# All units of the residual product of both residual attention layers issued ahead of the first tile of the aggregation

## The chip, the cores and the metric

The kernel runs on one core of a Trainium2 chip, as one launch. A core has a matrix engine (TensorE, PE in the profile), a vector engine (VectorE, DVE), a scalar engine (ScalarE, ACT), GpSimd (POOL) and a queue engine that issues transfers (SyncE, SP). Each runs its own instruction stream in order; streams meet only at semaphores. The metric is the device time of one execution in microseconds, the median over the runs shown.

## The reference

A chain of four graph networks over 625 nodes with 768 features; each adds its result to its input and normalises the rows. The first is a relational convolution, the second a plain graph convolution; the change touches neither. The third has two attention layers with a residual product each, and the change is there:

```python
h = gat_conv(x, edge_index, W1, a_src1, a_dst1, b1, HEADS, HID, True)      # 4 heads of 256
h = relu(layer_norm(h, g1, be1)) + (h0 @ Wr1 + br1)                        # residual product, 768 x 1024
h1 = h
h = gat_conv(h, edge_index, W2, a_src2, a_dst2, b2, 1, OUT_DIM, False)     # 1 head of 768
h = layer_norm(h, g2, be2) + (h1 @ Wr2 + br2)                              # residual product, 1024 x 768
# gat_conv: softmax over the edges that end in a node of leaky_relu(alpha_src + alpha_dst),
# then the sum of the source nodes' feature rows with these weights
```

The fourth network has two attention layers without a residual product (Q2 and Q3 in the kernel).

## The kernel before

Nodes are cut into NB = 5 blocks of BP = 125. Products in full precision are made of three matmuls on halves of the operands (high times low weight, low times high, high times high; lines 2060, 2063, 2064). Weights come as chunks of 128 rows by up to 384 columns through a ring of ten slots: SP loads a chunk, ACT makes its high half (`split_hi`, line 1065), POOL its low half (`split_to`, line 766), and PE waits for the low half and reports a used slot with `w_used`.

The two residual layers are the objects Q0 (first layer, 4 heads) and Q1 (second layer, 1 head). In each, PE goes through these steps:

- the feature product, with the attention scores beside it;
- the residual product in **units** (`residual_unit`): one unit is one block of nodes times one column piece. Q0 has 15 units of 6 chunks, i.e. 18 matmuls (units 0 to 9 are 384 columns wide, 10 to 14 are 256), Q1 has 10 units of 8 chunks, 24 matmuls. Q0's units use PSUM banks 3 and 4 in turn up to unit 9, and bank 3 alone from unit 10; Q1's alternate to the end. ACT copies a finished unit from its bank to `resid` (`residual_read`, line 1135), and POOL adds a bias row (`q0_residual`, line 806) or the layer's input (`q1_residual`, line 840);
- the aggregation in **tiles**: a tile of scores is a head and a block of nodes (20 in Q0, 5 in Q1). DVE writes the tile (`steep_or_flat`, line 1885), PE transposes its five blocks (`turn_tile`, line 2475), ACT takes exponentials in PSUM (`exps`, line 1087), DVE multiplies with the edge counts (`probs`, line 1848), and PE sums (`sum_tile`, line 2486: 5 matmuls for a Q0 tile, 10 for a Q1 tile). DVE inverts the row sum (`z`, line 1857), and ACT copies the scaled sum out (`out_scaled`, line 1148).

In Q0, PE turns tile j + 3 right after it sums tile j; DVE makes the last part of a tile's probabilities only after the sum of the tile before. After every fourth tile a block of nodes is complete: DVE takes statistics, ACT a square root (its table and that of the exponential are loaded in turn, lines 1026 and 1087) and the normalisation (line 1032), POOL multiplies by the gain (`q0_gain`, line 797), DVE adds and makes the layer's output (`q0_out`, lines 1874 and 1876). From tile 13 on PE also transposes the finished blocks for Q1 (`turn_x8`, line 2527), six of them through bank 4 alone, each after DVE has read the one before (line 1862). In Q1, each tile completes a block: read, statistics, square root, normalisation, gain (line 845), addition of the residual (line 1930), a second normalisation, and the transpose for Q2 (`turn_x2`, line 2049), which PE has between the two units of a later tile.

Before the change, PE has units 0 to 3 of Q0 ahead of the first tile, and the others each behind a tile, as a table says; in Q1 units 0 to 4 stand ahead and one unit before each tile. ACT's reads and POOL's additions follow that order by hand:

```python
Q0_BESIDE = {0: (4,), 1: (5,), 2: (6,), 3: (7,), 4: (8,), 5: (9,), 6: (10,), 7: (11,), 8: (12,), 10: (13,), 12: (14,)}
```

A queue limit matters: POOL splits the weight chunks of the second piece after it has added to unit 4 and those of the third after unit 9; ACT splits high halves just before it reads units 4, 9 and 14.

## Time and profile before

| | |
|---|---|
| time before, three runs | 1610.96 us median (1610.59 to 1614.87) |
| profiled execution, its own time | 1607.97 us |
| its span in the trace | 1606.2 us |
| mean granted clock of TensorE | 0.954 of full speed |
| busy: PE, DVE, POOL, ACT | 1464.7, 791.7, 506.6, 427.4 us |
| Q0's tile loop up to the sum of tile 13 | 1059.14 to 1134.87 us |
| Q0's tiles 13 to 19, with the transposes for Q1 | 1134.87 to 1181.56 us |
| Q1's units 0 to 5, then its tile loop | 1244.53 to 1270.23, 1270.23 to 1321.49 us |

Times are microseconds from the span's start. "Busy" is the time in which an engine has an instruction running; PE's matmuls overlap, so a matmul's duration is longer than the distance to the next start, and distances between starts are what a sequence costs. "PEclk" is the clock that TensorE was granted, 1.00 being 2.4 GHz and 0.50 being 1.2 GHz.

### The profile page before, as it was taken

Reading aid. Unit: us, or ns where it says so; the run is one execution under the profiler, and the core shown is the slowest. Engines: PE = TensorE matmul, PEld = TensorE weight load, DVE = VectorE, ACT = ScalarE, POOL = GpSimd, SP = SyncE. Lnnn points to the kernel's source line nnn. Section 1 sums busy time; section 2 is a strip of 40 time slices with the busy share of each in tenths; the row PEclk is TensorE's granted clock in tenths of the full one; section 3 lists DMA queues with packets and bytes.
Section 4 is the critical chain, followed back from the end, with each engine's and each line's share of the span. In section 5 each row is a group of like instructions: output and inputs, shape, how many; then the busy total and the mean of one; then the engine's idle time right before and its main releaser. Section 6 shows DMA issues by size and latency. Waiting matters only on the chain.

```text
span 1606.2 us, 23414 instructions
## 1 busy us (share of the span) xinstructions
PE 1464.7 (91%) x8072; PEld 1343.7 (84%) x8072; DVE 791.7 (49%) x1940; ACT 427.4 (27%) x1009; POOL 506.6 (32%) x586
## 2 busy tenths in 40 slices
PE   5899699999999999999999998999688998878896
PEld 3566699999999999999998997898578867767773
DVE  7889644224443365642324435534534043678524
ACT  1153511111000001101003113345524333544422
POOL 5110332423334424434342420633226534100020
PEclk9999899999999999999999998999889999777998
DMA  3110111213343243422112211310012102000001
GB/s 113 41 30 9 37 45 30 60 32 82 89 132 105 63 116 84 123 74 60 55 50 59 60 30 41 87 58 26 20 47 81 49 5 84 16 1 1 10 1 48
DMA packets 57656, 86.53 MB, mean 54 GB/s; under 512 B 6442, under 2 KB 54183, under 8 KB 57433
## 3 DMA queue, kind: packets, MB, share of 16 engines
q1 hardware_dynamic: 45184, 66.02, 14.3%
q10 hardware_dynamic: 12374, 19.17, 4.1%
q8 instruction: 66, 1.08, 0.3%
q14 instruction: 32, 0.26, 0.1%
HBM read 83.24 MB, written 1.92 MB: 53 GB/s over the span
## 4 chain that ended last, share of the span: by engine, by line
PE 74%; DVE 14%; ACT 5%; issue 4%; POOL 1%; DMA 1%; DVEq 0%; ACTq 0%; SPq 0%; POOLq 0%
PE psum L2060 13%; PE psum L2064 12%; PE psum L2063 12%; PE psum L2486 7%; PE psum L2077 7%; PE psum L2080 7%; PE psum L2165 2%; PE psum L2401 1%; PE psum L2406 1%; PE psum L2405 1%; ACT psum L1087 1%; DVE onehot_dst L1370 1%; PE psum L2121 1%; PE psum L2475 1%; PE psum L2457 1%
## 5 line engine op out<-in xcount | busy, mean ns | idle before, releaser
L2060 PE MATMUL psum<-w_lo,xT_hi 128*125 128x384 f32 (+2 forms) x1200 | 412.1, 343 | 11.7 <-POOL w_lo L766 5.3
L2063 PE MATMUL psum<-w_hi,xT_lo 128*125 128x384 f32 (+2 forms) x1200 | 405.5, 338 | 0.0
L2064 PE MATMUL psum<-w_hi,xT_hi 128*125 128x384 f32 (+2 forms) x1200 | 405.0, 337 | 0.0
L753 POOL CAST w_hi<-w_raw 128x384 fp32r<-128x384 f32 x190 | 103.3, 544 | 502.4 <-PE psum L2064 492.3
L2060 PEld LDWEIGHTS psum<-w_lo,xT_hi 128*125 128x125 f32 (+1 forms) x1200 | 225.0, 187 | 16.5 <-POOL w_lo L766 8.3
L766 POOL TENSOR_TENSOR w_lo<-w_raw,w_hi 128x384 fp32r<-128x384 f32 x106 | 109.8, 1065 | 387.9 <-ACT w_hi L1065 277.1
L2063 PEld LDWEIGHTS psum<-w_hi,xT_lo 128*125 128x125 f32 (+1 forms) x1200 | 225.4, 188 | 0.1
L2064 PEld LDWEIGHTS psum<-w_hi,xT_hi 128*125 128x125 f32 (+1 forms) x1200 | 224.8, 187 | 0.0
L1406 DVE TENSOR_TENSOR h_lo<-psum,h_hi 125x384 fp32r<-125x384 f32 (+1 forms) x120 | 66.9, 558 | 316.1 <-ACT h_hi L923 315.1
L2077 PE MATMUL psum<-h_lo,adjacency 125*125 125x384 f32 (+3 forms) x600 | 204.1, 340 | 1.8 <-ACT adjacency L963 1.7
L755 POOL TENSOR_TENSOR w_lo<-w_raw,w_hi 128x384 fp32r<-128x384 f32 x190 | 200.8, 1057 | 15.2
L923 ACT ACTIVATE h_hi<-psum 125x384 fp32r<-125x384 f32 (+1 forms) x120 | 59.0, 491 | 545.3 <-PE psum L2064 540.9
L2080 PE MATMUL psum<-h_hi,adjacency 125*125 125x384 f32 (+3 forms) x600 | 203.4, 339 | 0.0
L2486 PE MATMUL psum<-features,score_tiles 125*125 125x257 f32 (+2 forms) x400 | 122.6, 461 | 4.4 <-DVEq L2012 3.1
L2077 PEld LDWEIGHTS psum<-h_lo,adjacency 125*125 125x125 f32 (+1 forms) x600 | 112.0, 187 | 3.2 <-ACT adjacency L963 2.3
L1087 ACT ACTIVATE psum<-psum,al_src_slope 125x125 f32<-125x125 f32 x350 | 94.7, 351 | 73.9 <-PE psum L2475 73.8
L2080 PEld LDWEIGHTS psum<-h_hi,adjacency 125*125 125x125 f32 (+1 forms) x600 | 112.5, 188 | 0.3
L2486 PEld LDWEIGHTS psum<-features,score_tiles 125*125 125x125 f32 x400 | 79.2, 202 | 36.6 <-issue 5.0
L2486 PE MATMUL psum<-features,more_tiles 125*125 125x97 f32 x400 | 68.5, 334 | 26.1 <-DVE more_tiles L1848 25.9
L2486 PEld LDWEIGHTS psum<-features,more_tiles 125*125 125x125 f32 x400 | 63.5, 246 | 30.1 <-DVE more_tiles L1848 30.0
L2165 PE MATMUL psum<-onehot_dst,onehot_src 128*125 128x512 bf16 x336 | 62.5, 326 | 6.3 <-DVE onehot_dst L1370 5.9
L1370 DVE TENSOR_SCALAR onehot_dst<-iota,dst_of_pair 128x625 bf16<-128x625 f16 x168 | 62.8, 410 | 9.7 <-PE psum L2165 9.7
(286 smaller groups left out, 2097.9 us busy)
## 6 DMA issues: line engine op xcount, KB each, us to landing
w_raw<-weights_dram SPq DMA_DIRECT2D x296, 192.0 KB, 2.4
score_w_raw<-weights_dram ACTq DMA_DIRECT2D x58, 192.0 KB, 2.9
x_nat<-x_dram SPq DMA_DIRECT2D x1, 1875.0 KB
x_residual<-x_dram SPq DMA_DIRECT2D x1, 1875.0 KB
out_dram<-x_residual SPq DMA_DIRECT2D x5, 375.0 KB
score_a_rows<-L_gnn_a_src_dram ACTq DMA_DIRECT2D x8, 192.0 KB, 3.4
score_a_rows<-L_gnn_a_dst_dram ACTq DMA_DIRECT2D x8, 192.0 KB, 5.1
rgcn_bias<-rgcn_bias_dram SPq DMA_DIRECT2D x1, 1125.0 KB
```

Source lines behind the costliest of these rows:

```text
L753: nc.gpsimd.tensor_copy(mem.wh[:, slot, :], mem.raw[:, raw_slot, :]).then_inc(w_hi_ready, 1)
L755: nc.gpsimd.tensor_tensor(mem.wl[:, slot, :], mem.raw[:, raw_slot, :], mem.wh[:, slot, :].bitcast(F32), ALU.subtract).then_inc(w_lo_ready, 1)
L766: nc.gpsimd.tensor_tensor(mem.wl[:, c % WRING, :], mem.raw[:, c % RAW, :], mem.wh[:, c % WRING, :].bitcast(F32), ALU.subtract).then_inc(w_ ...
L1087: ins = nc.scalar.activation(t, t, ACT.Exp, bias=mem.al_src2[0:BP, n % NB, h:h + 1])
L1370: nc.vector.tensor_scalar(mem.oh_dst[:, n % OH_RING, 0:N], mem.iota[:, 0:N], mem.dst_pair[:, s % 2, j:j + 1], None, ALU.is_equal).then_inc ...
L2060: ins = nc.tensor.matmul(o, h, wl, start=(j == 0), stop=False, skip_group_check=True)
L2063: nc.tensor.matmul(o, l, wh, start=False, stop=False, skip_group_check=True)
L2064: ins = nc.tensor.matmul(o, h, wh, start=False, stop=stop and j == k - 1, skip_group_check=True)
L2077: ins = nc.tensor.matmul(o, a, mem.hl[0:p, slot, 0:width], start=(s == 0), stop=False, skip_group_check=True)
L2080: ins = nc.tensor.matmul(o, a, mem.hh[0:p, slot, 0:width], start=False, stop=(s == NB - 1), skip_group_check=True)
L2165: ins = nc.tensor.matmul(o, mem.oh_src[:, t, 0:BP], mem.oh_dst[:, n % OH_RING, w:w + 512 if w == 0 else NC], start=False, stop=(t == GROUP ...
L2486: ins = nc.tensor.matmul(bank(q.out_bank(u), off, off + width), blocks(p_tile(q, j))[:, k, :], feat_flat(q, k, a, a + width), start=(k == ...
```

## The change

On PE, units 4 to 14 of Q0 now stand between unit 3 and the sum of tile 0, and the table goes; units 5 to 9 of Q1 all stand ahead of its tile 0. ACT reads the units in the same new order, and has one group of high halves at tile 8 rather than 17. POOL adds to all units first, then splits, then has the gains.

```diff
@@ POOL
             for i in range(NB * len(Q0.pieces)):
-                if i == 10:
-                    q0_gain(0)
-                elif i == 13:
-                    q0_gain(1)
                 q0_residual(i)
                 if i == 4:
                     split_to(Q0.chunk + 32)
                 elif i == 9:
                     split_to(Q0.end)
             split_to(Q0.end + 4)
-            q0_gain(2)
-            q0_gain(3)
+            for b in range(3):
+                q0_gain(b)
             split_to(Q0.end + AHEAD)
-            q0_gain(4)
+            for b in range(3, NB):
+                q0_gain(b)
...
             for b in range(NB):
                 q1_residual(b)
-                if b:
-                    q1_gain(b - 1)
             split_to(Q1.end + 4)
+            for b in range(NB - 1):
+                q1_gain(b)
             q1_gain(NB - 1)
@@ ACT
-            residual_read(Q0, 2)
-            residual_read(Q0, 3)
+            for i in range(2, NB * len(Q0.pieces)):
+                residual_read(Q0, i)
...
-                for i in Q0_BESIDE.get(j, ()):
-                    residual_read(Q0, i)
...
-                if j == 17:
+                if j == 8:
                     split_hi(Q0.end + AHEAD)
...
-            for i in range(NB):
+            for i in range(2 * NB):
                 residual_read(Q1, i)
             for s in range(NB + 2):
                 if s < NB:
-                    residual_read(Q1, NB + s)
                     q1_read(s, 0)
@@ PE
-            for i, tiles in ((0, (0, 1)), (1, (2,)), (2, ()), (3, ())):
+            for i in range(NB * len(Q0.pieces)):
                 residual_unit(Q0, mem.xh, mem.xl, i)
-                for j in tiles:
-                    turn_tile(Q0, j)
+                if i == 0:
+                    turn_tile(Q0, 0)
+                    turn_tile(Q0, 1)
+                elif i == 1:
+                    turn_tile(Q0, 2)
             for j in range(4 * NB):
                 sum_tile(Q0, j)
                 if j + 3 < 4 * NB:
                     turn_tile(Q0, j + 3)
-                for i in Q0_BESIDE.get(j, ()):
-                    residual_unit(Q0, mem.xh, mem.xl, i)
...
+            for i in range(NB, 2 * NB):
+                residual_unit(Q1, mem.xh8, mem.xl8, i)
             for b in range(NB):
-                residual_unit(Q1, mem.xh8, mem.xl8, NB + b)
                 sum_tile(Q1, b, (lambda: turn_x2(b - 2)) if b >= 2 else None)
```

PE's rows in Q0, from the sum of tile 0 on. Before, the sum and the transposes of tile 3 are followed by the 18 matmuls of unit 4 (the first four are shown):

```order
L2486 MATMUL psum<-features,score_tiles 125x257 [waits feat_biased,gemm_read,prob_ready]
L2486 MATMUL psum<-features,score_tiles 125x257 x4
L2475 MATMUL psum<-ident,score_tiles 125x125 [waits g_ready]
L2475 MATMUL psum<-ident,score_tiles 125x125 [waits prob_ready]
L2475 MATMUL psum<-ident,score_tiles 125x125 x3
L2060 MATMUL psum<-w_lo,xT_hi 125x384 [waits gemm_read]
L2063 MATMUL psum<-w_hi,xT_lo 125x384
L2064 MATMUL psum<-w_hi,xT_hi 125x384
L2060 MATMUL psum<-w_lo,xT_hi 125x384
```

With the change, the last matmuls of unit 14 stand ahead of the same sum, and the tiles' rows follow each other with no product between them:

```order
L2053 MATMUL psum<-w_lo,xT_hi 125x256
L2056 MATMUL psum<-w_hi,xT_lo 125x256
L2057 MATMUL psum<-w_hi,xT_hi 125x256
L2479 MATMUL psum<-features,score_tiles 125x257 [waits feat_biased,gemm_read,prob_ready]
L2479 MATMUL psum<-features,score_tiles 125x257 x4
L2468 MATMUL psum<-ident,score_tiles 125x125 [waits g_ready]
L2468 MATMUL psum<-ident,score_tiles 125x125 [waits prob_ready]
L2468 MATMUL psum<-ident,score_tiles 125x125 x3
L2479 MATMUL psum<-features,score_tiles 125x257 [waits prob_ready]
L2479 MATMUL psum<-features,score_tiles 125x257 x4
L2468 MATMUL psum<-ident,score_tiles 125x125 [waits prob_ready,g_ready]
```

So 11 units, 198 matmuls, moved from behind tiles 0 to 8, 10 and 12 to ahead of tile 0; each sum now waits on `prob_ready` right behind the transposes.

POOL's rows in Q0, from the additions to units 0 to 4 (`br_first`) on. Before, two gains stand among the additions:

```order
L806 TENSOR_TENSOR residual_product<-residual_product,br_first 125x384 [waits gemm_read] x5
L766 TENSOR_TENSOR w_lo<-w_raw,w_hi 128x384 [waits w_hi_ready] x6
L806 TENSOR_TENSOR residual_product<-residual_product,br_rest 125x384 [waits br1_loaded,gemm_read]
L806 TENSOR_TENSOR residual_product<-residual_product,br_rest 125x384 [waits gemm_read] x4
L766 TENSOR_TENSOR w_lo<-w_raw,w_hi 128x384 [waits w_hi_ready] x4
L797 TENSOR_TENSOR dest_even<-dest_even,par_141 125x1024 [waits normed2]
L806 TENSOR_TENSOR residual_product<-residual_product,br_rest 125x256 [waits gemm_read] x3
L797 TENSOR_TENSOR par_142<-par_142,par_141 125x1024 [waits normed2]
L806 TENSOR_TENSOR residual_product<-residual_product,br_rest 125x256 [waits gemm_read] x2
```

With the change:

```order
L805 TENSOR_TENSOR residual_product<-residual_product,br_first 125x384 [waits gemm_read] x5
L765 TENSOR_TENSOR w_lo<-w_raw,w_hi 128x384 [waits w_hi_ready] x6
L805 TENSOR_TENSOR residual_product<-residual_product,br_rest 125x384 [waits br1_loaded,gemm_read]
L805 TENSOR_TENSOR residual_product<-residual_product,br_rest 125x384 [waits gemm_read] x4
L765 TENSOR_TENSOR w_lo<-w_raw,w_hi 128x384 [waits w_hi_ready] x4
L805 TENSOR_TENSOR residual_product<-residual_product,br_rest 125x256 [waits gemm_read] x5
L765 TENSOR_TENSOR w_lo<-w_raw,w_hi 128x384 [waits w_hi_ready] x4
L796 TENSOR_TENSOR dest_even<-dest_even,par_141 125x1024 [waits normed2]
```

The gains moved behind all additions; the two groups of low halves (`w_lo`, x6 and x4) stay behind the additions to units 4 and 9 in both.

## Rows read from the trace of the kernel before

**Rows 1.** Busy time by stage: length, each engine's busy time, granted clock, DMA.

```profile
1059.14:1134.87 75.73, 70.18 (x395) 63.42 (x394) 32.07 (x72) 40.54 (x112) 24.68 (x23) 0.95 0.11 34
1134.87:1181.56 46.69, 28.85 (x117) 23.24 (x115) 15.97 (x36) 20.23 (x47) 14.26 (x12) 0.78 0.14 38
...
1244.53:1270.23 25.70, 25.66 (x145) 25.34 (x146) 0.87 (x2) 7.56 (x19) 16.32 (x14) 1.00 0.23 64
1270.23:1321.49 51.26, 51.26 (x215) 37.15 (x214) 18.32 (x56) 20.78 (x39) 15.76 (x9) 1.00 0.02 7
1321.49:1340.16 18.67, 10.21 (x49) 9.24 (x50) 10.39 (x23) 7.26 (x15) 12.32 (x11) 0.82 0.32 91
```

**Rows 2.** PE's longest group of waits from 1059 to 1182 us: total, times, longest.

```profile
PE psum L2527 <- DVE x8T_lo L1862: 17.4, 5, 4.8
```

**Rows 3.** Timeline of PE in Q0's tile loop: start, length, instruction, idle before.

```profile
1061.78 0.42 PE L2060 MATMUL psum<-w_lo,xT_hi 128*125 128x384 f32 x1
...
1065.01 2.33 PE L2486 MATMUL psum<-features,score_tiles 125*125 125x257 f32 x10
...
1103.15 0.57 PE L2060 MATMUL psum<-w_lo,xT_hi 128*125 128x256 f32 x1 [2.83 <-POOL w_lo L766]
...
1106.82 3.50 PE L2486 MATMUL psum<-features,score_tiles 125*125 125x257 f32 x10
...
1110.62 0.36 PE L2060 MATMUL psum<-w_lo,xT_hi 128*125 128x256 f32 x1
...
1112.83 2.33 PE L2486 MATMUL psum<-features,score_tiles 125*125 125x257 f32 x10
...
1117.68 2.33 PE L2486 MATMUL psum<-features,score_tiles 125*125 125x257 f32 x10
...
1121.12 2.33 PE L2486 MATMUL psum<-features,score_tiles 125*125 125x257 f32 x10
...
1138.74 2.33 PE L2486 MATMUL psum<-features,score_tiles 125*125 125x257 f32 x10
...
1144.85 2.33 PE L2486 MATMUL psum<-features,score_tiles 125*125 125x257 f32 x10
...
1152.02 4.49 PE L2486 MATMUL psum<-features,score_tiles 125*125 125x257 f32 x10
```

**Rows 4.** Timeline of POOL at unit 4's addition and the splits behind it.

```profile
1066.74 1.00 POOL L806 TENSOR_TENSOR residual_product<-residual_product,br_first 125x384 f32<-125x384 f32 x1 [5.84 <-ACT residual_product L1135]
1067.70 5.12 POOL L766 TENSOR_TENSOR w_lo<-w_raw,w_hi 128x384 fp32r<-128x384 f32 x5
```

**Rows 5.** Timeline of DVE: the end of a block, score tiles, probabilities.

```profile
1112.33 1.23 DVE L1876 SCALAR_TENSOR_TENSOR residual_product<-dest_even,residual_product 125x1024 f32<-125x1024 f32 x1
...
1117.00 0.61 DVE L1885 TENSOR_SCALAR score_tiles<-score_tiles,row_steep,row_flat 125x625 f32<-125x625 f32 x1
...
1124.77 2.33 DVE L1885 TENSOR_SCALAR score_tiles<-score_tiles,row_steep,row_flat 125x625 f32<-125x625 f32 x1
...
1128.42 0.72 DVE L1848 SCALAR_TENSOR_TENSOR score_tiles<-psum,counts_loops 125x125 f32<-125x125 f32 x2
```

**Rows 6.** Timelines of ACT and POOL: the second block's square root, normalisation and gain.

```profile
1118.28 1.28 ACT L1026 ACT_TABLE_LOAD   x1
...
1123.04 1.25 ACT L1032 ACTIVATE par<-par,ln_shift,ln_std 125x1024 f32<-125x1024 f32 x1
1124.37 2.38 POOL L797 TENSOR_TENSOR par<-par,par 125x1024 f32<-125x1024 f32 x1 [5.31 <-ACT par L1032]
```

**Rows 7.** Timeline of ACT in Q1: tile 3's first read, and the last normalisations of tiles 3 and 4.

```profile
1306.88 0.58 ACT L1148 ACTIVATE x_residual<-psum,z 125x384 f32<-125x384 f32 x1 [1.93 <-POOL residual_product L840]
...
1315.16 1.03 ACT L1032 ACTIVATE x_residual<-x_residual,ln_shift,ln_std 125x768 f32<-125x768 f32 x1 [0.42 <-DVE ln_shift L1513]
...
1329.62 1.03 ACT L1032 ACTIVATE x_residual<-x_residual,ln_shift,ln_std 125x768 f32<-125x768 f32 x1 [0.43 <-DVE ln_shift L1513]
```

**Rows 8.** Busy time from 1117 to 1134 us, columns as in Rows 1.

```profile
1117.00:1134.00 17.00, 15.60 (x97) 13.80 (x96) 11.96 (x26) 11.77 (x32) 4.03 (x3) 1.00 0.01 1
```

More of the change, by code:

```diff
@@ L607, in program @@
         X8_BANKS = [4] * 6 + [5, 6, 7, 4]
-        Q0_BESIDE = {0: (4,), 1: (5,), 2: (6,), 3: (7,), 4: (8,), 5: (9,), 6: (10,), 7: (11,), 8: (12,), 10: (13,), 12: (14,)}
         X8_AT = {13: 0, 14: 1, 15: 2, 16: 3, 17: 4, 18: 5, 20: 6, 21: 7, 24: 8, 25: 9}
```

## The prediction

> **What bounds the kernel now.** I read the stages first, and asked of each that the change touches whether PE works or waits there, then the list of PE's waits, then the timelines. Q0's loop up to the sum of tile 13 lasts 75.73 us, and PE is busy for 70.18 of them. The next six tiles take 46.69 us with PE busy for 28.85 at a mean clock of 0.78: there PE waits. In Q1 PE has no gap at all in units 0 to 5 (25.70 us) and in the tile loop behind them (51.26 us); then come 18.67 us with PE busy for 10.21 [rows 1]. PE's waits say on what: 17.4 us in five waits of the transposes for Q1 for the reader of bank 4 [rows 2], all from tile 14 on; the longest single wait before that is 2.83 us on a low half of the weights, at unit 10 [rows 3]. So units between tiles are what fills PE while DVE and ACT work on the scores. The change takes no work away; it takes this filling from where there is other work to wait for.
>
> **Q0, units 4 to 14 ahead of tile 0.** A 384-wide unit costs 3.23 us from start to start (1061.78 to 1065.01), a 256-wide one 2.21 (1110.62 to 1112.83) [rows 3]: 6 x 3.23 + 5 x 2.21 = 30.4 us, the same as before. What is added:
> - Low halves at unit 5. POOL adds to unit 4 (1.0 us) before it splits chunks 26 to 29, at 1.02 us each [rows 4]. ACT's read first, about 0.6: the first half is there 2.6 us after unit 4, the fourth 5.7, and three matmuls (0.5) end unit 5 at 6.3 instead of 3.2. Wait 3.1 us. Before, a tile lay between and took most of it.
> - The same at unit 10. From unit 9's start, ACT and POOL need 2.0 us for the split that POOL has before its additions; five additions take it to 7, the four splits to 11.1, the last matmuls to 11.5. Without waits units 9 and 10 take 5.4. Wait 6.1 us. Before, with a tile between, the longest piece of it was 2.83 [rows 3].
> - Bank 3 alone for units 10 to 14: each of the last four must let ACT read its predecessor, 0.4 us and two hand-overs, 0.65 us. Four times: 2.6 us, between 0 and 4.
> - The clock. Behind the wait of 2.83 us the sum of tile 7 took 3.50 us rather than 2.33 [rows 3]: TensorE was at 1.2 GHz. Behind a wait of about 4 us the same falls on units 10 to 12: 2 us, between 0 and 5.
>
> The new stretch ahead of tile 0: 30.4 + 3.1 + 6.1 + 2.6 + 2.0 = 44.2 us.
>
> **Q0, tiles 0 to 12 bare.** PE's own work for a tile is the sum and five transposes, 2.64 us (from tile 0's sum at 1059.14 to unit 4 at 1061.78) [rows 1, 3]. The rest of the loop sets a longer beat. (a) DVE makes a tile's last probabilities after the sum of the tile before: a sum starts 2.33 us for its predecessor, a hand-over, the inverse and the first of two parts of 0.36 [rows 5] after the last one, about 2.8. (b) Every fourth tile the last transpose waits for a bank: tile 9 to tile 10, which had no unit between, took 3.44 us (1117.68 to 1121.12) [rows 3]. Four plain tiles: 2.85 + 3.44 + 2.63 + 2.8 = 11.7 us. (c) Once a block is complete, ACT loads a table (1.28 us), takes the root, loads the other table (1.28), makes exponentials and normalises (1.25); POOL multiplies (2.38); DVE needs two operations of 1.2 and only then writes the next score tile (0.61), on which PE's transposes wait [rows 5, 6]. I walked tiles 4 to 12 through the four queues with these durations: exponentials come 0.8 us late at the third tile behind a block's end, and at the fourth DVE's output is 1.4 us late for the transposes. Tiles 4 to 7 take 12.5 us, 8 to 11 take 13.7, tile 12 takes 4.2. Sum 11.7 + 12.5 + 13.7 + 4.2 = 42.1 us, 3.24 a tile. Bounds: 2.63 a tile, PE's own work (34.2), and 3.87 a tile, the step from tile 13's sum (1134.87, the end of the stretch) to tile 14's at 1138.74, which holds a transpose for Q1 too (50.3) [rows 1, 3]. I take the walk; it lies between (a) and the measured 3.87.
>
> Q0 to tile 13: 44.2 + 42.1 = 86.3 against 75.73: **+10.6 us**. The six tiles after it depend on the same chain as before; ACT comes 0.8 us later into it: **+0.8**. ACT's five high halves at tile 8 (2.2 us) and POOL's splits between gains lie in slack there and cost nothing; if tile 8's exponentials were late for them, it would be 2 us.
>
> The Trainium skill has a rule on this loop (SBUF — State Buffer, Who interferes with whom): DVE and GpSimd share a port pair, and the one that comes second is blocked for the other's whole instruction. The trace agrees: a score tile took 2.33 us beside POOL's gain and 0.61 otherwise [rows 5, 6]. By it, POOL's additions leaving the loop would relieve DVE, while a gain that fell beside each block's score tile would cost 1.7 us four times. My walk has DVE waiting for the gain, so neither is added.
>
> **Q1, units 5 to 9 ahead.** Six units took 25.70 us [rows 1], 4.28 each, so tile 0 starts 4 x 4.22 = 16.9 us later; the work is PE's either way. A tile then costs PE 6.4 to 6.9 us instead of 11. But each completes a block, and its chain is serial: from ACT's first read (1306.88) through turns, statistics, two normalisations and the second read to the end of the last normalisation (1316.19) is 9.3 us, the gain beside it [rows 7]. Before, that hid beneath 11 us of PE. Now from tile 0's start: last normalisation of tile 0 at 10.3, of tile 1 at 19.5, then 9.3 a tile, of tile 4 at 47.4. That is 16.9 + 47.4 = 64.3 us from the old start of the loop (1270.23), where it was at 60.4 (1329.62 + 1.03) [rows 7]: **+3.9 us**, and what follows (splits, turns, products of Q2) hangs on it as before. Bounds: 0, if all of it hides, and 9.3, if one more beat is missed. The longer gaps, up to 5 us, may leave the products behind them at 1.2 GHz: **+1**, between 0 and 3.5.
>
> Weights: Q1's second piece is asked for at the same place as before, and POOL's additions no longer stand before tiles 1 to 4. SP's queue only follows the low halves. Costless.
>
> **Sum.** 10.6 + 0.8 + 3.9 + 1.0 = 16.3 us. The profiled execution took 1607.97 us, so 1624.3; the median of the runs shown is 3.0 higher, so I forecast **1627 us**. A change within 0.3%, 4.8 us, is about what a measurement of this kernel can't tell from none.
>
> **Rivals.**
> - *TensorE falls to half clock in the bare loop.* A sum at 1.2 GHz is the 4.49 us of 1152.02, 2.2 more than at 2.4 GHz [rows 3]. If half of the 13 tiles run so: +14 us, 1641. For it: the loop would have PE idle a fifth of the time, and the six tiles that are already bare have 0.78. Against: 1117 to 1134 had PE idle for 1.4 of 17 us and stayed at 1.00 [rows 8]. Chance 0.17. The Trainium skill (TensorE: Matmul & The Clock Gate, A second HAM failure mode) describes just this, frequent short idling between groups of matmuls making the clock swing; no full-clock row here has as much idling as the new loop.
> - *Hidden anyway, no change.* The bare loop runs at PE's 2.63 a tile (-7.9 us), the clock holds (-3), and Q1's chain hides (-3.9): +1.5, 1612. Against: (a) and (b) are order, not luck. Chance 0.09.
> - *Faster.* The six tiles 13 to 18 take 46.69 us, and the clock's mean there is 0.78 [rows 1]; the step at full clock from 1138.74 to 1144.85 was 6.1 us [rows 3]. If the clock held in all six, they would take 37: -10 us. The place is PE's wait for bank 4's reader, and it decides only where the rest costs less than 5 us. Together with the hidden case's bare loop: 16.3 - 10 - 7.9 - 3 = -4.6 or beyond, 1606. Against: nothing in the change shortens these waits. Chance 0.04.
> - *My mechanism,* 0.70, own range 1616 to 1637: the low end from 2.9 us a tile (-4.4), the clock (-3), and two or three of the waits ahead halved (-4); the high end from banks and clock (+5) and one more missed beat in Q1 (+5).
>
> **How the numbers follow.** Slower by over 0.3%: 0.17 + the mechanism's 0.70 but for a sliver of 0.02 = 0.85; within: 0.09 + 0.02 = 0.11; faster 0.04. For 8 in 10, I leave out half of the half-clock case and most of the two below: 1614 to 1640.
>
> **What would show it.** In the profile after: a wait of PE on POOL's low halves of about 4 us at unit 10, and one near 2 us at unit 5; 44 us from unit 4's start to tile 0's sum; sums of tiles 0 to 12 some 3.2 us apart, with waits of the transposes on DVE; a granted clock near 1.00 there; tiles 13 to 19 near 47 us; no unit among Q1's tiles, ACT's last normalisations 9.3 us apart, and the turns of the last block waiting longer than 0.78 us for ACT. Wrong it would be if DVE and ACT kept up with PE's 2.63 us, if the clock fell in the bare loop, or if the waits at 13 to 19 moved with the clock by more than all of the above.

## The result, and the profile after

The changed kernel takes **1635.77 us** (median of 4 runs, 1629.02 to 1640.11) against 1610.96 us before (median of 4 runs, 1610.59 to 1614.87): ratio 1.0145, 95% interval 1.0104 to 1.0186. Timed again in 5 rounds (`after_again`, below) it took 1632.63 us, ratio 1.0129, 1.0114 to 1.0145; the experiments are compared with that, since its interval is narrower. Both lie above the forecast of 1627 us and inside its range, on the side that was forecast.

The profiled execution took 1640.11 us (span 1638.4, 1606.2 before). Stages of the kernel after, columns as in [rows 1]: Q0's units 4 to 14 ahead of tile 0; tiles 0 to 12; tiles 13 to 19; the work between Q0's and Q1's loops; Q1's ten units; Q1's five tiles up to the last turn for the next layer.

```profile
1060.90:1105.17 44.27, 36.30 (x201) 33.03 (x200) 0.00 (x0) 10.76 (x25) 19.43 (x21) 0.88 0.16 46
1105.17:1153.44 48.27, 40.98 (x197) 34.13 (x195) 31.26 (x68) 31.28 (x87) 9.52 (x7) 0.93 0.09 27
1153.44:1202.80 49.36, 30.60 (x115) 24.81 (x115) 17.70 (x41) 19.06 (x47) 9.71 (x7) 0.76 0.07 20
1202.80:1269.25 66.45, 59.54 (x341) 54.77 (x339) 30.11 (x46) 23.61 (x58) 28.32 (x22) 0.94 0.20 62
1269.25:1311.81 42.56, 42.51 (x241) 42.19 (x242) 0.87 (x2) 11.19 (x27) 23.73 (x18) 1.00 0.17 47
1311.81:1368.26 56.45, 47.19 (x162) 30.77 (x162) 27.48 (x78) 24.02 (x45) 20.26 (x15) 0.91 0.10 28
```

The first two stages together last 92.5 us. What answers to them before is the 75.73 us of [rows 1]: +16.8 us. Tiles 13 to 19 have gone from 46.69 to 49.36, +2.7. Q1 runs without a gap through its ten units, as forecast; the work that was beside its tiles is simply earlier.

PE's waits after, one line per waiting instruction and releaser (total us, times, longest), in four stretches: units ahead, tiles 0 to 12, tiles 13 to 19, Q1's tiles.

```profile
PE psum L2053 <- POOL w_lo L765: 6.1, 5, 4.0
PE psum L2053 <- ACT residual_product L1131: 1.9, 4, 0.5
...
PE psum L2468 <- DVE score_tiles L1878: 5.8, 2, 4.0
...
PE psum L2520 <- DVE x8T_lo L1855: 18.3, 5, 5.1
...
PE psum L2042 <- ACT x_residual L1028: 7.3, 3, 3.5
```

The two lines of the units ahead are the waits that the prediction had at units 5 and 10 and at bank 3. The third is new: PE's transposes (L2468, formerly L2475) wait for a score tile of VectorE. The fourth answers to [rows 2], 18.3 us for 17.4. The timeline of PE after shows what each wait leaves behind it:

```profile
1066.85 0.44 PE L2053 MATMUL psum<-w_lo,xT_hi 128*125 128x384 f32 x1 [1.57 <-POOL w_lo L765]
...
1067.81 0.44 PE L2053 MATMUL psum<-w_lo,xT_hi 128*125 128x384 f32 x1 [0.17 <-POOL w_lo L765]
...
1087.83 0.58 PE L2053 MATMUL psum<-w_lo,xT_hi 128*125 128x256 f32 x1 [3.98 <-POOL w_lo L765]
...
1088.79 0.58 PE L2053 MATMUL psum<-w_lo,xT_hi 128*125 128x256 f32 x1
...
1090.72 0.58 PE L2053 MATMUL psum<-w_lo,xT_hi 128*125 128x256 f32 x1
...
1092.20 0.57 PE L2053 MATMUL psum<-w_lo,xT_hi 128*125 128x256 f32 x1 [0.47 <-ACT residual_product L1131]
...
1096.87 0.58 PE L2053 MATMUL psum<-w_lo,xT_hi 128*125 128x256 f32 x1 [0.47 <-ACT residual_product L1131]
...
1100.07 0.38 PE L2053 MATMUL psum<-w_lo,xT_hi 128*125 128x256 f32 x1 [0.47 <-ACT residual_product L1131]
...
1102.93 0.38 PE L2053 MATMUL psum<-w_lo,xT_hi 128*125 128x256 f32 x1 [0.47 <-ACT residual_product L1131]
...
1130.54 0.81 PE L2468 MATMUL psum<-ident,score_tiles 125*125 125x125 f32 x5 [1.84 <-DVE score_tiles L1878]
1131.19 3.90 PE L2479 MATMUL psum<-features,score_tiles 125*125 125x257 f32 x10
...
1148.20 0.84 PE L2468 MATMUL psum<-ident,score_tiles 125*125 125x125 f32 x5 [3.95 <-DVE score_tiles L1878]
1148.85 4.02 PE L2479 MATMUL psum<-features,score_tiles 125*125 125x257 f32 x10
```

The sums behind 1.84 and 3.95 us of idleness (those of tiles 8 and 12) take 3.90 and 4.02 us where the others take 2.33 to 2.43 [rows 3]. The steps from them to the next sum are 4.48 and 4.59 us, where the steps at the same place in the blocks before, from tiles 0 and 4, are 2.91 and 3.00: the lower clock adds some 1.5 us to each wait. Two windows (the first reaches from the wait at unit 10 to the start of unit 12, the second is the slow sum of tile 8 with the transposes behind it) show the granted clock:

```profile
1087.83:1096.87 9.04, 8.09 (x30) 6.73 (x30) 0.00 (x0) 0.77 (x2) 3.57 (x4) 0.50 0.31 87
1131.19:1135.70 4.51, 4.51 (x18) 3.60 (x16) 3.46 (x7) 1.30 (x5) 0.00 (x0) 0.62 0.01 4
```

In the first window it is 0.50, that is 1.2 GHz, throughout. What this costs is read from starts. The chunks of unit 10 begin 0.96 us apart (1087.83, 1088.79), exactly as those of unit 5 did at full clock (1066.85, 1067.81): POOL's splits set that pace, and the lower clock adds nothing there. It adds 0.3 us in the last chunk of unit 10 (from 1090.72), 1.8 us in unit 11 (4.67 us from 1092.20 to 1096.87, against 2.86 us for unit 13 from 1100.07 to 1102.93, each with one wait for the bank) and 0.3 us in unit 12 (3.20 us): about 2.5 us.

Why VectorE's score tile is late is seen on the other engines' timelines after (start, length, instruction, idle before):

```profile
1124.20 0.60 DVE L1878 TENSOR_SCALAR score_tiles<-score_tiles,row_steep,row_flat 125x625 f32<-125x625 f32 x1
...
1127.80 2.69 DVE L1878 TENSOR_SCALAR score_tiles<-score_tiles,row_steep,row_flat 125x625 f32<-125x625 f32 x1
...
1144.27 0.68 DVE L1841 SCALAR_TENSOR_TENSOR score_tiles<-psum,counts_loops 125x500 f32<-125x500 f32 x1 [2.52 <-PE psum L2479]
...
1145.46 2.68 DVE L1878 TENSOR_SCALAR score_tiles<-score_tiles,row_steep,row_flat 125x625 f32<-125x625 f32 x1
...
1127.80 2.34 POOL L796 TENSOR_TENSOR dest_even<-dest_even,par 125x1024 f32<-125x1024 f32 x1 [17.14 <-ACT dest_even L1028]
1145.47 2.34 POOL L796 TENSOR_TENSOR par<-par,par 125x1024 f32<-125x1024 f32 x1 [15.32 <-ACT par L1028]
...
1139.30 2.16 ACT L1061 ACTIVATE w_hi<-w_raw 128x384 fp32r<-128x384 f32 x5
1141.36 0.45 ACT L1144 ACTIVATE dest_even<-psum,z 125x256 f32<-125x256 f32 x1
1141.83 1.28 ACT L1083 ACT_TABLE_LOAD   x1
1143.13 1.11 ACT L1083 ACTIVATE psum<-psum,al_src_slope 125x125 f32<-125x125 f32 x4
```

Two causes stand here. POOL's gain begins within 0.01 us of the score tile both times, and the score tile then lasts 2.69 and 2.68 us instead of 0.60; the first ends at 1130.49, 0.35 us after the gain. And at tile 8 ACT's five high halves (2.16 us) stand ahead of the read of tile 9 and of the second table load, so that the exponentials come at 1143.13. The wait of DVE at 1144.27 is put down to PE, but PE's sum of tile 10 was long done (DVE had its inverse from it at 1141.58): what came last were these exponentials.

### The profile page after: what moved, and what is told of

Read it like the earlier page. It is cut to its first block, busy times and chain, and to the rows that moved or that the text cites. A ratio compares the mean times of both kernels' runs of the same rounds, so it can differ in the third digit from the quotient of the medians.

```text
span 1638.4 us, 23414 instructions
## 1 busy us (share of the span) xinstructions
PE 1480.5 (90%) x8072; PEld 1354.6 (83%) x8072; DVE 793.3 (48%) x1940; ACT 428.4 (26%) x1009; POOL 506.0 (31%) x586
## 3 DMA queue, kind: packets, MB, share of 16 engines
q1 hardware_dynamic: 45184, 66.02, 13.8%
## 4 chain that ended last, share of the span: by engine, by line
PE 74%; DVE 14%; ACT 5%; issue 3%; POOL 2%; DMA 1%; DVEq 0%; ACTq 0%; SPq 0%; POOLq 0%
PE psum L2053 13%; PE psum L2056 13%; PE psum L2057 13%; PE psum L2479 8%; PE psum L2070 7%; PE psum L2073 7%; PE psum L2158 2%; PE psum L2394 1%; PE psum L2468 1%; PE psum L2399 1%; PE psum L2398 1%; DVE onehot_dst L1363 1%; PE psum L2450 1%; ACT psum L1083 1%; PE psum L2114 1%
## 5 line engine op out<-in xcount | busy, mean ns | idle before, releaser
L2479 PE MATMUL psum<-features,score_tiles 125*125 125x257 f32 (+2 forms) x400 | 127.2, 476 | 4.5 <-DVEq L2005 3.1
L2468 PE MATMUL psum<-ident,score_tiles 125*125 125x125 f32 x350 | 60.9, 313 | 11.8 <-DVE score_tiles L1878 9.9
L1850 DVE RECIPROCAL z<-psum 125x1 f32<-125x1 f32 x25 | 4.2, 166 | 133.6 <-PE psum L2479 133.6
```

Source lines behind the costliest of these rows:

```text
L2468: nc.tensor.transpose(turned_part(q, v, n, n + 1), g_tile(q, j)[:, nodes(c)], mem.ident[0:BP, 0:BP]).then_inc(g_turned, 1)
L2479: ins = nc.tensor.matmul(bank(q.out_bank(u), off, off + width), blocks(p_tile(q, j))[:, k, :], feat_flat(q, k, a, a + width), start=(k == ...
```

## Experiments

All were timed in 5 rounds beside the kernel before on the same chip; the groups (the first four runs, the next four, the first three of the last section, and its fourth) were on different chips, so runs of different groups are compared by their ratios. Differences in us are the ratio's difference times 1611, unless medians are named.

### Which layer costs it: Q0's part alone, Q1's part alone

Q0 alone is the change without its lines for Q1; Q1 alone is these on the kernel before:

```
+            for i in range(NB, 2 * NB):
+                residual_unit(Q1, mem.xh8, mem.xl8, i)
             for b in range(NB):
-                residual_unit(Q1, mem.xh8, mem.xl8, NB + b)
```

with ACT's reads and POOL's gains moved as in the change.

> The change made in Q0 alone; Q1's units, reads and gains stand as before. Theory A (latency: the bare tile loops of both layers can't keep TensorE busy, Q0 costs 11 to 20 us, Q1 about 4): 10 to 20 us slower than before, 1621 to 1631. Rival B (the loss is all in Q1's serial chain or in the clock at large): within 5 us of before. If the two layers add up, this and the Q1-only kernel together give the whole change.

> The change made in Q1 alone; Q0 as before. Theory A: 4 to 5 us slower (1615), with ACT's last normalisations 9.3 us apart and no gap of TensorE during the ten units. Rival B: 10 us or more slower. Rival C (Q1's chain hides anyway): within 2 us of before.

Q0 alone: 1628.98 us (1626.71 to 1630.99), ratio 1.0102 (1.0086 to 1.0119), 16.4 us. Q1 alone: 1615.49 us (1611.38 to 1622.24), ratio 1.0020 (1.0007 to 1.0034), 3.2 us. The two add up to 19.6; the whole change cost 20.8 in its second timing. Within the intervals the two parts add, and Q0's is five sixths of their sum. Q1's tiles in the run with Q1 alone:

```profile
1290.19:1346.33 56.14, 45.30 (x161) 29.62 (x161) 27.46 (x78) 24.01 (x45) 20.25 (x15) 0.94 0.09 26
```

It is close to the 56.45 us of the changed kernel; before, the same tiles with their units took 69.05. They gave back 12.9 us, and the units ahead took 16.9, which leaves 4.0.

### ACT's high halves back at tile 17

```
-                if j == 8:
+                if j == 17:
                     split_hi(Q0.end + AHEAD)
```

In POOL's order four gains instead of three stand before the five low halves.

> The changed kernel, with ACT's five high halves back at tile 17 and POOL's five low halves back behind the fourth gain. Theory A (those 2.2 us of ACT at tile 8 make the second block's chain late): the wait of the transposes before the sum of tile 12 falls from 3.95 us to about 2, and the kernel is 2 to 4 us faster than the changed one. Rival B (the wait is the block's chain and the shared port, and the halves lay in slack): no difference, the wait stays near 4.

1627.19 us (1625.44 to 1628.97), ratio 1.0093 (1.0077 to 1.0109): 5.8 us better than the changed kernel, more than the 2 to 4 expected. The step from tile 11 to 12 is 4.86 us in place of 6.93, and PE's waits in tiles 0 to 12 are:

```profile
PE psum L2467 <- DVE score_tiles L1877: 4.4, 3, 1.9
```

The wait of 3.95 is down to 1.88, the other of 1.84 stays at 1.83, and a third of 0.65 is new, ahead of tile 13. The sum behind 1.83 again took 4.02 us, the one behind 1.88 only 2.33. Tiles 0 to 12 took 45.3 us, 2.9 less. The rest came in tiles 13 to 19, 45.1 us for 49.4; that part did not come back in the run with both repairs (48.1), so it is not to be counted on; PE's clock there differs between executions.

### The stretch ahead repaired: POOL's splits first, two banks

```
+                if i == 4:
+                    split_to(Q0.chunk + 31)
+                elif i == 5:
+                    split_to(Q0.end)
                 q0_residual(i)
-                if i == 4:
-                    split_to(Q0.chunk + 32)
-                elif i == 9:
-                    split_to(Q0.end)
...
-            self.banks = list(range(NB)) * n + [4 if i % 2 and (i < 10 or heads == 1) else 3 for i in range(NB * n)]
+            self.banks = list(range(NB)) * n + [4 if i % 2 else 3 for i in range(NB * n)]
```

The splits stand ahead of the additions of units 4 and 5, and units 10 to 14 use banks 3 and 4 by turns instead of bank 3 (the first turn for the next layer waits for unit 13's reader accordingly).

> The changed kernel, with POOL's splits of Q0's second and third piece ahead of its additions to units 4 and 5, and units 10 to 14 in banks 3 and 4 in turn. It takes away what the change adds ahead of tile 0 (predicted 3.1 + 6.1 + 2.6 + 2 us) and leaves the bare loop. Theory A (the bare loop costs as much again): from unit 4 to tile 0's sum about 33 us rather than 44, and the kernel 8 to 11 us faster than the changed one, still 10 us or more slower than before. Rival B (the loss is the waits ahead): as fast as before.

1619.95 us (1617.50 to 1623.81), ratio 1.0052 (1.0035 to 1.0069): 12.4 us better than the changed kernel and 8.4 behind the one before, where 8 to 11 better and 10 or more behind were expected. The window from the first turn to tile 0's sum, and PE's waits in it:

```profile
1047.87:1089.97 42.10, 41.42 (x267) 40.87 (x268) 3.11 (x6) 16.15 (x41) 22.68 (x24) 1.00 0.17 51
```

```profile
PE psum L2053 <- POOL w_lo L765: 0.7, 2, 0.3
```

In the changed kernel the same window takes 55.43 us with PE busy for 47.46. So 13.3 us went; the terms that the prediction had added for this stretch come to 13.8. The profile books 7.3 of them as idle and 6.0 as busy, but the 6.0 are not all clock: the starts give some 2.5 us for it, and in unit 10 PE's slower matmuls fill time in which it would have waited for POOL anyway. Tiles 0 to 12 took 48.4 us, as in the changed kernel: the loop's own waits (1.83 and 3.93 us) don't depend on the stretch ahead.

### The gain: nearly none, and on another engine; and the changed kernel again

The first keeps the operation and its wait but multiplies only 8 columns:

```
-  nc.gpsimd.tensor_tensor(dest0(b), dest0(b), mem.par[1][0:BP, :], ALU.mult).then_inc(gained, 1)
+  nc.gpsimd.tensor_tensor(dest0(b)[:, 0:8], dest0(b)[:, 0:8], mem.par[1][0:BP, 0:8], ALU.mult).then_inc(gained, 1)
```

The second puts the whole product into VectorE's `q0_out`, ahead of the bias.

> The changed kernel with GpSimd's gain of Q0 on 8 of its 1,250 columns; the multiplication of the other columns is left out, so the output is not the reference's. Theory 1 (the gain of 2.34 us stands beside a score tile of VectorE, which then takes 2.7 us in place of 0.6, and so the turns wait 1.84 us at 1130.54 and 3.95 us at 1148.20): both waits shrink to under 0.7 us, the sums behind them go back to 2.7 us, and tiles 0 to 12 take 43 to 45 us in place of 48.3; the kernel is 3 to 6 us faster than the changed one. Rival (the five high halves and the norm on ScalarE make the second wait, by making all of tile 8's chain late): the wait at 1148.20 stays over 2 us and only the first goes; 1 to 2 us faster. Second rival (the score tile is late for its inputs and would be late with a short gain too): no change.

> The changed kernel with the gain of Q0 moved from GpSimd to VectorE, in the same chunk of work as the addition of the bias (so some 1.2 us more on VectorE for each of four tiles, and one hop between engines less). Theory 1 (VectorE's score tile is slowed by GpSimd's gain beside it): no score tile takes over 1 us, the 4 x 1.7 us that go are a bit more than the 4 x 1.2 us that come, and they come at a place where three score tiles are ready ahead; tiles 0 to 12 take 44 to 47 us, the kernel is 1 to 4 us faster than the changed one. Rival (VectorE's total work in this stretch decides, not where the score tile stands): no difference of over 1 us.

> The changed kernel itself once more, on the same chip as these three, since its own four runs spread over 11 us and three versions of it have come out 8 to 16 us faster. If its 1635.8 us are its time, it comes out at 1633 to 1638 and the three stages before the loop of Q0, between Q0 and Q1, and behind Q1 are late again (some 1.8, 3.5 and 3.3 us) though nothing in them is changed. If they are the spread of single runs, it comes out at 1626 to 1632, and the differences of the versions to it shrink by as much.

(A tile has 1,024 columns in the rows of the profile; the number of columns in the first expectation is wrong, the edit is as shown.)

Short gain: 1628.50 us (1626.51 to 1629.91), 1.0110 (1.0095 to 1.0126). The changed kernel again: 1632.63 (1630.71 to 1635.85), 1.0129 (1.0114 to 1.0145). The medians are 4.1 us apart (the ratios 3.1), and the intervals just overlap; the profile has the same 4.1 us in tiles 0 to 12, 44.08 us for 48.22. Score tile and waits in the run with the short gain:

```profile
1128.04 0.59 DVE L1878 TENSOR_SCALAR score_tiles<-score_tiles,row_steep,row_flat 125x625 f32<-125x625 f32 x1
```

```profile
PE psum L2468 <- DVE score_tiles L1878: 2.6, 2, 1.7
```

With no long gain beside it the score tile takes 0.59 us again. Of the 5.8 us of waits 2.6 are left (0.93 and 1.68), not under 0.7 each as expected: the short gain and the high halves each took 2.3 and 2.1 us out of the wait of 3.95, so it had both causes. The sum behind the wait of 1.68 still took 4.02 us.

Gain on VectorE: 1633.95 us (1631.71 to 1634.91), 1.0141 (1.0125 to 1.0156): no gain over the changed kernel in time, where 1 to 4 us were expected. In the profiled execution tiles 0 to 12 took 46.8 us, 1.4 less than in the changed kernel again and inside the 44 to 47 of the first theory. No score tile stands beside a gain any more (the longest, at 1140.42, takes 1.32 us, where under 1 was expected), but VectorE's own queue shows what came instead:

```profile
1131.49 1.21 DVE L1863 TENSOR_TENSOR dest_even<-dest_even,par 125x1024 f32<-125x1024 f32 x1
1132.73 1.23 DVE L1864 TENSOR_TENSOR dest_even<-dest_even,par 125x1024 f32<-125x1024 f32 x1
1134.00 1.23 DVE L1866 SCALAR_TENSOR_TENSOR residual_product<-dest_even,residual_product 125x1024 f32<-125x1024 f32 x1
```

Three wide operations stand in a row ahead of the next score tile (at 1135.14). The waits moved to other tiles, 6.3 us in three (2.19, 1.69 and 2.42). By the time measured the rival was right: VectorE's total work in this stretch counts.

The changed kernel again had tiles and units as in the first profile (first turn to tile 0's sum 55.5, tiles 0 to 12 48.2, tiles 13 to 19 49.4 us), while what lay outside moved: its first turn came 2.5 us later, and the stretch from Q1's first product to its first sum was 107.3 us for 109.0. Behind Q1's last turn for the next layer it took 265.3 us for 270.1 (266.9 before). So some 2 to 5 us of a single execution lie in stages that the change does not touch.

### Both repairs at once

> The changed kernel with both repairs at once: ScalarE's high halves back at tile 17 and GpSimd's splits ahead of the additions, with two banks in turn for units 10 to 14. If the two causes add: tile 0's first sum comes 42 us after the first turn, as in the run with the ahead-stretch repaired, and tiles 0 to 18 take what they took with the high halves at 17; that is 1620 less 2 to 5, so 1615 to 1618 us, still 3 to 6 us behind the kernel before. Rival (the high halves at tile 17 are worth the 8.6 us that their run was ahead of the changed one): 1611 to 1612, level with the kernel before. Rival 2 (they hide each other, since the half clock that follows one delay covers the other): 1619 to 1621.

1616.68 us (1611.91 to 1620.57), 1.0030 (1.0016 to 1.0044): 16 us of the 20.8 are gone, as expected. Its three stages of Q0 (first turn to tile 0's sum, tiles 0 to 12, tiles 13 to 19):

```profile
1049.55:1091.64 42.09, 41.40 (x268) 40.85 (x268) 3.11 (x6) 16.18 (x41) 22.68 (x24) 1.00 0.18 51
1091.64:1136.96 45.32, 39.48 (x197) 32.96 (x196) 31.42 (x69) 29.41 (x83) 9.52 (x7) 0.96 0.09 29
1136.96:1185.08 48.12, 29.71 (x117) 24.05 (x115) 16.74 (x41) 20.84 (x51) 9.47 (x7) 0.80 0.07 21
```

Their sum is 135.5 us; before it was 133.6 (11.2, 75.73 and 46.69), in the changed kernel again 153.1. With the repairs, having all units of Q0 ahead costs 1.9 us in these stages. Of that, units and tiles 0 to 12 together are 0.5 us: 30.9 us more ahead of tile 0 and 45.3 for the bare tiles, against 75.73 for both in one loop. The kernel before had none of the repairs, so this sets a repaired order against an unrepaired one.

### Two banks for the turns of x8

PE's 17.4 us of [rows 2] are all of one kind: the next turn waits until VectorE has read bank 4. Bank 3 lies free there once unit 14 is read.

```
-        X8_BANKS = [4] * 6 + [5, 6, 7, 4]
+        X8_BANKS = [4, 3] * 3 + [5, 6, 7, 4]
...
+                if n == 1:
+                    pe.wait_ge(gemm_read, Q0.gemm0 + NB * len(Q0.pieces) + 15)
```

The first run has this alone in the kernel before, the second POOL's splits first as well, the third all units of both layers ahead with both repairs and the two banks, and the fourth the same with Q1 as before.

> The kernel before with the turns of x8 that stand in the loop in banks 4 and 3 by turns in place of bank 4 alone. In the rows of before TensorE stands 17.4 us in five of them for VectorE's low half of the turn before, which frees bank 4, and runs some sums behind them at 1.2 GHz (4.5 us in place of 2.3). Theory (the bank is what closes this chain): these waits fall to under 5 us in all and tiles 13 to 19 take 36 to 42 us in place of 46.7, the kernel is 5 to 10 us faster than before. Rival (ScalarE and VectorE, with the norms, three table loads and the exponentials, set the pace there, and the bank only shows it): the waits turn up at the sums or the turns of score tiles, and the kernel is within 2 us of before.

> The same, and GpSimd's splits of the last chunks ahead of the five additions at unit 9, so that unit 10 finds its weights: the wait of 2.83 us at 1103.15 of before goes. If it is on the path, 2 to 3 us faster than the run with the two banks alone; if tile 7 to 10's chain on VectorE and ScalarE takes it back, under 1 us.

> All residual units ahead, as in the changed kernel, with both repairs (high halves at tile 17, GpSimd's splits first, units 10 to 14 in two banks) and the two banks for the turns of x8. If the two banks are worth in this order what they are in that of before (5 to 10 us), it comes out at 1607 to 1612 us, and 4 to 6 us behind the same edit in the kernel before: then the order ahead is what costs, not something that stood beside it. If the order ahead leaves ScalarE and VectorE more behind at tile 13 (score tiles and exponentials late), the two banks bring less, 0 to 4 us.

> The run with all units ahead, both repairs and two banks for the turns of x8, with Q1 in the order of before again: only Q0's units are ahead. By the PE rows of the two runs before it, Q0 took 114.5 us from its first turn to the first product of the next layer with the units ahead and 113.1 us with them beside the tiles, and the rest of their 6.6 us lay in Q1 and behind it. If so, this one comes out at 1592 to 1594 us, 4 to 6 us faster than with Q1's units ahead too and 1 to 3 us behind the two banks in the order of before. Rival (Q1's order is worth only the 3.4 us that it cost by itself in the kernel before, and 2 to 3 us lie in Q0 in single runs that the profiled execution does not show): 1594 to 1596 us.

| kernel | us, median (runs) | ratio to before, 95% | Q0's three stages, us |
|---|---|---|---|
| two banks, order of before | 1591.39 (1587.95 to 1593.54) | 0.9879, 0.9863 to 0.9894 | 11.2 + 75.8 + 26.1 |
| and splits first | 1589.94 (1588.22 to 1592.71) | 0.9867, 0.9852 to 0.9882 | 11.2 + 73.9 + 26.4 |
| all ahead, repaired, two banks | 1598.02 (1594.99 to 1598.52) | 0.9907, 0.9894 to 0.9921 | 42.1 + 45.4 + 27.0 |
| the same, Q0 only | 1593.34 (1592.08 to 1594.12) | 0.9880, 0.9864 to 0.9897 | 42.1 + 45.3 + 27.0 |

Windows of tiles 0 to 12 and 13 to 19 in the first of them, PE's waits in the second window, and the timeline around tile 15:

```profile
1059.65:1135.44 75.79, 70.20 (x395) 63.42 (x395) 32.08 (x72) 40.61 (x112) 24.69 (x23) 0.95 0.11 34
1135.44:1161.52 26.08, 20.97 (x117) 17.41 (x115) 15.28 (x36) 20.25 (x47) 10.85 (x9) 1.00 0.11 31
```

```profile
PE psum L2527 <- DVE x8T_lo L1862: 3.2, 2, 2.1
```

```profile
1142.02 0.59 PE L2527 MATMUL psum<-ident,residual_product 125*128 125x125 f32 x4
1142.44 2.33 PE L2486 MATMUL psum<-features,score_tiles 125*125 125x257 f32 x10
```

26.1 us instead of 46.7: the waits fell from 17.4 to 3.2, and PE's busy time for the same work from 28.85 to 20.97, at a clock of 1.00 instead of 0.78. I had expected half of this gain (5 to 10 us): I had counted the waits and not the clock behind them. The second of these turns, at 1142.02, goes out at once; before it waited for 2.79 us, and sums of 4.41 to 4.49 us followed behind later waits of 3.43 to 4.81 us (the first of them in [rows 3]). All ahead with both repairs and the two banks came out at 1598.02 us where 1607 to 1612 were expected, and 6.6 us behind the same edit in the order of before for 4 to 6; the fourth run hit its 1592 to 1594. The splits first remove PE's wait of 2.83 us in unit 10, but a later transpose (at 1113.42) then waits 3.62 us for a score tile (the step from tile 8's sum to tile 9's is 9.71 us there, 4.85 before), and the timed difference of 1.9 us is inside the intervals.

With the two banks the order ahead of Q0 alone is level with the order beside (0.9880 and 0.9879; the stages differ by 1.4 us). Against the second run, which has POOL's splits first as it has, it is 2.1 us behind, inside the intervals, and 2.9 in the stages. Q1's part costs another 4.3 us there, as it cost 3.2 in the kernel before.

## Why the prediction was right, and where its terms were off

**Side: right. Mechanism: right ahead of tile 0 and in Q1, wrong in Q0's loop.** The prediction made Q0's loss out of waits ahead of tile 0 (+13.8) and let the bare tiles give 3.2 us back: 42.1 us, where the loop before took 45.3 beside its 30.4 us of units. The first held. The second did not: the bare tiles took 48.3. With the high halves at tile 17 they took 45.3, no more and no less than before, so what the loop lost was not the filling as such.

**The stretch ahead of tile 0: 44.2 us forecast, 44.3 measured, term by term.** Read from starts, as the sum was: units 4 and 5 took 9.45 us instead of 6.46 (wait at unit 5: 3.0, forecast 3.1); unit 10 took 9.2 us instead of 2.2, of which 0.65 are the bank and 0.3 the clock (wait at unit 10: 6.0, forecast 6.1); units 11 to 14 each began 0.65 us late for the bank (2.6, forecast 2.6); the clock took 2.5 (forecast 2.0); units 6 to 9 together were 0.3 us quicker than at 3.23 us each. The profile's list of waits shows less, 2.1, 4.0 and 1.9, since a wait begins there only where the modelled end of the last matmul lies, and since the slower matmuls of unit 10 cover part of the wait for POOL. PE's busy time of 36.30 us for 30.4 us of work is therefore not a price of the clock.

**Tiles 0 to 12: 42.1 us forecast, 48.3 measured. This is the step that failed.** By blocks:

| | forecast | measured |
|---|---|---|
| tiles 0 to 3 | 11.7 | 11.9 |
| tiles 4 to 7 | 12.5 | 14.1 |
| tiles 8 to 11 | 13.7 | 17.7 |
| tile 12 | 4.2 | 4.6 |

The beats (a) and (b) held: steps of 2.7 to 3.0 us, and 3.5 at every fourth. Two sentences did not hold. "My walk has DVE waiting for the gain, so neither is added": the score tile of the tile ahead stood beside the gain both times, at 2.69 and 2.68 us. The run with the short gain, where the score tile is back at 0.59 us, shows that the gain makes it; priced at 1.7 us each time, it would have given 3.4 of the 6.2 us. The Trainium skill (SBUF — State Buffer, Who interferes with whom) states that DVE in its two-port modes and GpSimd exclude each other for a whole instruction, whoever issues first, and that a tensor_scalar, as L1878 is, can enter these modes; the prediction had named this rule and left it out of its sum. The trace agrees in the length of the delay; which of the two issued first it does not tell (1127.80 for both; 1145.46 for DVE, 1145.47 for GpSimd), and it was DVE that was held. And "ACT's five high halves at tile 8 (2.2 us) and POOL's splits between gains lie in slack there and cost nothing; if tile 8's exponentials were late for them, it would be 2 us": they were late, and it was 2.07 us at the step to tile 12 and 2.9 over the stage. I had named the place and the price and taken the wrong branch. Some 1.5 us of half clock behind each of the two waits is in the measured blocks, and not in the forecast, which looked for a clock near 1.00 there.

**Tiles 13 to 19: +0.8 forecast, +2.7 measured.** The waits on the turns rose by 0.9 us (18.3 for 17.4) and PE's busy time by 1.75, at a clock of 0.76 for 0.78. With both repairs it is +1.4.

**Q1: +4.9 forecast, +4.3 in the profile** (from the first unit to the last turn 99.0 us; before 94.75) and 3.2 in the timed run of Q1 alone. The working held by parts: the units took 16.9 us more, ACT's normalisations of one kind came 9.24 to 9.26 us apart, and the one that answers to the last of [rows 7] ended 47.25 us after tile 0's start for 47.4 forecast:

```profile
1358.03 1.03 ACT L1028 ACTIVATE x_residual<-x_residual,ln_shift,ln_std 125x768 f32<-125x768 f32 x1 [0.42 <-DVE ln_shift L1506]
```

In both kernels this row is the first of tile 4's two normalisations and not, as [rows 7] and the prediction call it, the last. The second begins at 1366.55 after and at 1338.20 before, and gives the same: 3.6 us later counted from the old start of the loop, against 3.7 by the first. One sign did not come: the last block's turn no longer waited for ACT. PE reached it 0.7 us after that normalisation had ended, with no gap before it.

**Not in the sum:** the stretch between the two loops took 66.45 us for 62.97, of which 1.7 were gone in the second profile. In all runs with Q0's change, the time from Q1's first product to Q1's first sum, less the 16.9 us of units where these are in it, is 1.7 to 3.5 us longer than the 88.7 us of before; but it is 2.3 us longer (91.0) with two banks in the order of before too. What it is stays open.

**The rivals.** Half clock in the bare loop did not come as drawn: the mean was 0.93, and two sums of thirteen, each behind a long wait, took about 4 us. "Hidden anyway" describes the repaired kernels: with the waits ahead, the high halves and the bank of the turns mended, Q0's order costs 1.4 to 2.9 us, and the bare loop takes 45.3 us, not 34. "Faster" asked that the clock hold in tiles 13 to 19, for 10 us: the place was right and worth 20 us, but it was a second bank that opened it, in either order, and not the change.

**Best version run:** the kernel before with two banks for the turns, 1591.39 us, or with the splits first as well, 1589.94; the two are not told apart.

## What to carry to other kernels

Where a matrix engine is moved away from work that filled its gaps, follow each of the other queues through the new order, with everything in it. Here the order of the weight splits on POOL and ACT, and one PSUM bank where two could be had, cost 16 of the 20.8 us, and the moved work itself some 2 in Q0 and 3 to 4 in Q1. A wait of TensorE can cost more than its length: the half clock behind it took 1.5 to 2.5 us where it came, and the length of the wait did not tell whether it would. Give the sum both ends, read what a clock costs from starts and not from busy time, and test it by removing the wait. And when a stage waits several times for the reader of one buffer while another lies free, mend that first: here it was worth as much as the whole change cost.

## What the runs showed of the hardware that was not expected

- A VectorE operation of 0.60 us that began within 0.01 us of a GpSimd one of 2.34 us took 2.69 and 2.68 us: it ended 0.35 and 0.33 us after the other. Beside a GpSimd operation on 8 columns it took 0.59.
- Behind an idle stretch of 3.98 us the granted clock was 0.50 for the following 9.04 us, although PE was busy for 8.09 of them. Behind waits of 1.68 (short gain), 1.84 and 3.95 us (changed kernel) the next sum took 3.9 to 4.0 us; behind waits of 1.88, 3.37 and 3.43 us (high halves at tile 17) and of 2.05 and 2.79 us (kernel before) it took 2.33. The length of a wait alone does not order these cases.
- Tiles 13 to 19 in the kernel with two banks had PE idle for 5.1 of 26.08 us, in gaps of at most 2.05 us, and stayed at 1.00.
- The same work of PE at tiles 13 to 19 took 20.97 us busy at 1.00, 28.85 at 0.78 and 30.60 at 0.76: a busy time read from a stage at a lower clock is not the work's price. Nor is its excess the clock's price: ahead of tile 0 it was 5.9 us, where the starts give 2.5.
